# Expert weights split into three buffers, and another order of the head of a four-layer kernel

## What is computed

```python
x = x + ssm(layernorm(x))          # complex diagonal state space, 64 states, scan over 512 tokens, D skip, W_out, b_out
x = x + experts(layernorm(x))      # 8 experts, top 2 of a router
x = x + attention(layernorm(x))    # 16 heads of 64, bias by relative position, softmax
x = x + experts(layernorm(x))      # the same weights once more

def experts(x):                    # x: 2048 tokens x 128
    logits = x @ router_w.T
    vals, idx = top_k(logits, 2)
    g = sigmoid(vals); g = g / (g.sum(-1) + 1e-10)
    out = 0
    for e in range(8):
        ge = sum(where(idx == e, g, 0), -1)
        out += ge[:, None] * ((silu(x @ w_gate[e]) * (x @ w_up[e])) @ w_down[e])
    return out
```

## Time and profile before

| | us |
|---|---|
| median of 3 runs | 932.55 (930.68 to 934.95) |
| the profiled execution | 934.97 |
| its span in the profile | 933.2 |
| TensorE busy | 833.9 (89%) |
| VectorE, ScalarE, GpSimd busy | 645.2, 527.9, 432.1 |
| mean granted TensorE clock | 0.952 of 2.4 GHz |

### The profile page before, as it was taken

One profiled execution on the slowest core, in us unless ns is written; L12 is line 12 of the kernel. 1 busy time (PEld: TensorE's weight loads), 2 busy tenths in 40 slices (PEclk: granted clock), 3 DMA queues, 4 the chain that ended last, 5 costly groups with the idle time before them and its releaser, 6 DMA issues. The chain is left out here.

```text
span 933.2 us, 13407 instructions
## 1 busy us (share of the span) xinstructions
PE 833.9 (89%) x4320; PEld 559.7 (60%) x4320; DVE 645.2 (69%) x1600; ACT 527.9 (57%) x1161; POOL 432.1 (46%) x454
## 2 busy tenths in 40 slices
PE   2977878988789999999999999999999976899887
PEld 1566666866655556556565565565655565677665
DVE  7686666756778776767766768767688474775666
ACT  4445344544466766665666666666666543454443
POOL 2532568867324333332433424333335242697765
PEclk9878989989999999999999999999999997998999
DMA  6001263264000000000000000000000301622301
GB/s 203 3 1 25 62 120 88 60 195 189 0 1 1 1 1 1 1 1 1 1 2 1 1 1 1 1 2 1 23 13 1 70 1 42 120 83 57 85 1 45
DMA packets 51140, 35.14 MB, mean 38 GB/s; under 512 B 2640, under 2 KB 48592, under 8 KB 51072
## 3 DMA queue, kind: packets, MB, share of 16 engines
q1 hardware_dynamic: 51072, 34.30, 14.0%
HBM read 33.04 MB, written 1.25 MB: 37 GB/s over the span
## 5 line engine op out<-in xcount | busy, mean ns | idle before, releaser
L1200 POOL TENSOR_SCALAR prob<-prob,inv_total 128x512 f32<-128x512 f32 x256 | 175.0, 697 | 309.7 <-DVE inv_total L967 309.7
L720 POOL TENSOR_TENSOR hid_lo<-hid,hid_hi 128x512 fp32r<-128x512 f32 x128 | 190.6, 1504 | 153.7 <-ACT hid_hi L543 151.6
L1106 ACT ACTIVATE prob<-prob,peak 128x512 f32<-128x512 f32 x256 | 185.9, 726 | 46.4 <-DVE peak L978 46.4
L978 DVE CUSTOM_DVE_ANT_0 prob<-bank,bias_band 128x512 f32<-128x512 f32 x256 | 166.5, 688 | 28.8 <-PE bank L870 22.9
L597 DVE TENSOR_TENSOR hid<-silu,bank 128x512 f32<-128x512 f32 x128 | 87.3, 684 | 107.2 <-PE bank L245 89.3
L536 ACT ACTIVATE silu<-bank 128x512 f32<-128x512 f32 x128 | 76.4, 598 | 123.3 <-PE bank L245 123.3
L243 PE MATMUL bank<-xT_hi,w_hi 128*128 128x512 f32 x256 | 110.9, 433 | 36.4 <-POOL w_lo L710 29.8
L899 PE MATMUL bank<-probT,v 128*64 128x512 f32 x512 | 137.4, 617 | 0.0
L881 PE MATMUL bank<-ident,prob 128*128 128x128 f32 x1024 | 134.3, 274 | 3.0 <-ACT probT L1112 1.8
L881 PEld LDWEIGHTS bank<-ident,prob 128*128 128x128 f32 x1024 | 118.1, 141 | 21.6 <-issue 5.4
L624 DVE TENSOR_TENSOR hid<-hid,gate_all 128x512 f32<-128x512 f32 x118 | 120.5, 1023 | 8.5 <-DMA gate_all<-gates 0.7
(11 more groups left out here) (156 smaller groups left out, 1269.9 us busy)
## 6 DMA issues: line engine op xcount, KB each, us to landing
gate_all<-gates SPq DMA_DIRECT2D x59, 256.0 KB, 5.6
bias_band<-bias_rows SPq DMA_DIRECT2D x16, 448.0 KB, 8.8
w_raw<-in_w_gate SPq DMA_DIRECT2D x16, 128.0 KB, 2.3
w_raw<-in_w_up SPq DMA_DIRECT2D x16, 128.0 KB, 2.4
w_raw<-in_w_down SPq DMA_DIRECT2D x16, 128.0 KB, 2.5
x_res<-in_x SPq DMA_DIRECT2D x4, 256.0 KB, 5.2
out<-x_res SPq DMA_DIRECT2D x4, 256.0 KB, 2.3
wqT<-in_WqT SPq DMA_DIRECT2D x1, 512.0 KB, 6.1
```

The lines of the kernel that those rows point to most:

```text
L720: nc.gpsimd.tensor_tensor(m["hid_lo"][:, pos % 2, half, :], m["hid"][:, pos % deep, half, :], m["hid_hi"][:, pos % 2, half, :].bitcast(F32 ...
L978: nc.vector.tensor_tensor_reduce(out=prob[:, buf, h, :], in0=bank[2 * (n % 2) + h][:, :], in1=row_bias, scale=-1.0, scalar=NEG_START, op0= ...
L1106: nc.scalar.activation(prob[:, buf, h, :], prob[:, buf, h, :], ACT.Exp, bias=peak[:, buf, h:h + 1], scale=-1.0, accum_out=total[:, buf, h: ...
L1200: nc.gpsimd.tensor_scalar(prob[:, buf, h, :], prob[:, buf, h, :], inv[:, buf, h:h + 1], 1.0, ALU.mult, ALU.mult).then_inc(a_n, 1)
```

## The change

The weights get a third slot for `w_hi` and `w_lo` (`W_BUFS = 3`, expert e in slot e % 3; `w_raw` keeps two), each slot a tensor of its own at an address that is free at the time. `SPLIT_AT` gives the step at which the first of an expert's three pieces is split, the others follow in the next two. Steps are numbered 0 to 31 through a layer (`ORDER`), and `hid` is used four slots deep throughout. In the second expert layer chunk 3 comes later in the first eight steps. SyncE loads the gates of expert e + 2 behind the step that used their slot, and the next weights behind the third piece.

In the head the queues are reordered: loads of x first, the attention's weights in four loads with semaphores of their own, the first pair's layer norm ahead of the angles; PE turns wq first. The states make one product of both PSUM banks with cosine and sine together and one of the state with both; GpSimd's cosine product and bias go, the bias becomes a matmul of a row of ones (`ssm_skip`), in which the skip product also goes ahead of the states. The order on VectorE is states 0, 1, 2, residual 0, states 3, residual 1, layer norm of the first two chunks, residuals 2 and 3. The first eight expert steps and the routing are interleaved in another order, and in `leave` chunk 3's transpose, logits and gates come later.

The diff, cut to its core:

```diff
+        turn = slot(4, 2).rearrange("p (r s) -> p r s", r=2)
+        ut = slot(6, 2).rearrange("p (r s) -> p r s", r=2)
+        zt = slot(10, 4).rearrange("p (b r s) -> p b r s", b=2, r=2)
...
-                           w_raw=R(56), routing=R(62), gate_all=R(68)),
+                           w_hi=[R(44), R(47), R(84)], w_lo=[R(50), R(53), R(41)], w_raw=R(56), routing=R(62),
+                           gate_all=R(68)),
...
+        LAST_CHUNK_LATE = [(0, 0), (0, 1), (1, 0), (1, 1), (0, 2), (1, 2), (0, 3), (1, 3)]
+        ORDER = [[(2 * i + par_, c) for i, pair in enumerate([first, BY_EXPERT, BY_EXPERT, BY_CHUNK]) for par_, c in pair]
+                 for first in (BY_CHUNK, LAST_CHUNK_LATE)]
...
+        W_BUFS = 3
+        DEEP = 4
+        SPLIT_AT = [[None, None, 3, 6, 10, 14, 18, 22], [None, None, 3, 7, 10, 14, 18, 22]]
...
+        def splits(k, s):
+            return [(e, s - SPLIT_AT[k][e]) for e in range(2, E) if 0 <= s - SPLIT_AT[k][e] < 3]
-        FIRST_PIECES = {6: [(0, 1, 0)], 7: [(0, 1, 1)]}
-        MIDDLE_PIECES = {0: [(0, 0, 2)], 1: [(1, 0, 0)], 2: [(1, 0, 1)], 3: [(1, 0, 2)], 6: [(0, 1, 0)],
-                         7: [(0, 1, 1)]}
-        LAST_PIECES = {0: [(0, 0, 2), (1, 0, 0)], 1: [(1, 0, 1)], 2: [(1, 0, 2)]}
...
+            if e >= W_BUFS:
+                if piece < 2:
+                    act.wait_ge(q["u"], 2 * LAST[k][e - W_BUFS] + 2)
                 else:
+                    act.wait_ge(q["d"], LAST[k][e - W_BUFS] + 1)
...
         def experts_sync(sp, k):
+            for s in range(STEPS_K):
+                e, c = ORDER[k][s]
+                if e + 2 < E:
+                    sp.wait_ge(q["gm"], 2 * s + 2)
+                    load_gates(sp, k, e + 2, c)
+                for after in range(2, E - 2):
+                    if s == SPLIT_AT[k][after] + 2:
+                        load_weights(sp, k, after + 2)
...
+            def enter():
+                down(pe, 0, STEPS_K - 2)
                 ln_turn(pe, 2, 0, 4)
-                down_30()
...
             def leave():
                 part(2, 0)
                 pe.wait_ge(a_ea, SLOTS)
+                down(pe, 1, 0)
                 part(2, 1)
-                ln_turn(pe, 3, 3, JOB_BANK)
                 part(3, 0)
                 pe.wait_ge(a_eb, SLOTS)
+                down(pe, 1, 1)
                 part(3, 1)
+                ln_turn(pe, 3, 3, JOB_BANK)
+                part(4, 0)
+                pe.wait_ge(a_o, B * PAIRS)
+                down(pe, 1, 2)
+                part(4, 1)
                 route_logits(pe, 1, 3, JOB_BANK)
+                expert_step(pe, 1, 5)
+                expert_step(pe, 1, 6)
                 route_turn(pe, 1, 1)
                 route_spread(pe, 1, 3)
+                expert_step(pe, 1, 7)
...
+            def ssm_skip(b):
+                nc.tensor.matmul(bank[4 + b][:, :], ones[0:1, :], bo[0:1, :].unsqueeze(1).to_broadcast([1, QT, D]),
+                                 start=True, stop=False, skip_group_check=True)
+                for n in range(QT):
+                    nc.tensor.matmul(bank[4 + b][:, n * P:(n + 1) * P], xf[:, xtok], wd[:, :], start=False, stop=False,
...
+            for c in (2, 3):
+                pe.wait_ge(LN[0]["hi"], c - 1)
+                ln_turn(pe, 0, c, c + 2)
+            ssm_in(2)
+            ssm_skip(0)
+            ssm_out(0)
+            pe.wait_ge(LN[0]["hi"], 4)
+            ssm_in(3)
+            ssm_skip(1)
+            ssm_out(1)
...
+            step = lambda s: [gate_up(pe, 0, s, half) for half in range(2)]
             route_logits(pe, 0, 0, 4)
+            step(0)
             route_logits(pe, 0, 1, 5)
+            step(1)
+            step(2)
             ln_turn(pe, 1, 2, 6)
+            route_spread(pe, 0, 0)
+            route_spread(pe, 0, 1)
+            pe.wait_ge(m_x, 4)
+            route_turn(pe, 0, 0)
+            pe.wait_ge(MOE[0]["gt_c"], 1)
             ln_turn(pe, 1, 3, 7)
+            step(3)
...
-            def turn_back(b):
-                nc.gpsimd.tensor_tensor(zc[:, b % 2, :], z[:, b % 2, :], cosT, ALU.mult).then_inc(m_zc, 1)
...
+            layer_norm_0(0)
             dve.wait_ge(ld_times, 16)
...
+                nc.vector.tensor_tensor(ut, psum[:, 2 * (b % 2):2 * (b % 2) + 2, :], turn, ALU.mult).then_inc(m_z, 1)
+                nc.vector.tensor_tensor(ut[:, 0, :], ut[:, 0, :], ut[:, 1, :], ALU.add).then_inc(m_z, 1)
+                nc.vector.tensor_tensor(zt[:, b % 2], z[:, b % 2, :].unsqueeze(1).to_broadcast([P, 2, S]), turn,
+                                        ALU.mult).then_inc(m_zt, 1)
...
             states(0)
             states(1)
+            states(2)
             residual(0)
-            states(2)
+            states(3)
             residual(1)
-            states(3)
             dve.wait_ge(m_x, 2)
             ln_rows(dve, 1, 0, 2)
```

More of the change, by code:

```diff
@@ L561, in scalar_step @@
+        def scalar_step(act, k, s):
             silu_of(act, k, s, 0)
-            high_of(act, k, s - 1, (pos - 1) % 8, 1, deep_before if pos == 0 else deep)
+            high_of(act, k, s - 1, 1)
             silu_of(act, k, s, 1)
-            high_of(act, k, s, pos, 0, deep)
-            for par_, ahead, piece in pieces.get(pos, ()):
-                weight_high(act, k, i, par_, ahead, piece)
+            high_of(act, k, s, 0)
+            for e, piece in splits(k, s):
+                weight_high(act, k, e, piece)
@@ L632, in vector_step @@
+        def vector_step(dve, k, s):
             for half in range(MT):
-                product(dve, k, s, pos, half, deep, first and pos < deep)
-                gated(dve, k, i, order, pos, half, deep, first)
+                product(dve, k, s, half)
+                gated(dve, k, s, half)
         def add_sums(dve, k, c):
@@ L716, in low_of @@
             q, m = MOE[k], MEM[k]
             pool.wait_ge(q["hi"], 2 * s + half + 1)
-            if not first:
+            if s >= 2:
                 pool.wait_ge(q["d"], s - 1)
-            nc.gpsimd.tensor_tensor(m["hid_lo"][:, pos % 2, half, :], m["hid"][:, pos % deep, half, :],
-                                    m["hid_hi"][:, pos % 2, half, :].bitcast(F32), ALU.subtract).then_inc(q["hl"], 1)
-        def pool_step(pool, k, i, pos, pieces, deep=2, first=False):
-            s = 8 * i + pos
-            low_of(pool, k, s, pos, 0, deep, first and pos < 2)
-            for par_, ahead, piece in pieces.get(pos, ()):
-                weight_low(pool, k, 2 * (i + ahead) + par_, par_, piece)
-            low_of(pool, k, s, pos, 1, deep, first and pos < 2)
@@ L743, in build @@
+        def experts_pool(pool, k):
+            for s in range(STEPS_K):
+                low_of(pool, k, s, 0)
+                for e, piece in splits(k, s):
+                    weight_low(pool, k, e, piece)
+                low_of(pool, k, s, 1)
+        A_BANK = [6, 7, 6, 7]
         PV_BANK, JOB_BANK = 6, 7
@@ L1430, in _ @@
+            for piece in range(3):
+                weight_high(act, 0, 1, piece)
+            act.wait_ge(ld_wv, 16)
+            nc.scalar.copy(wvh[:, :], wv[:, :]).then_inc(s_ah, 1)
+            silu = lambda s: [silu_of(act, 0, s, half) for half in range(2)]
+            cast = lambda s: [high_of(act, 0, s, half) for half in range(2)]
             ln_apply(act, 1, 0, 0)
```

693 lines of the change are left out of this document (299 added, 394 removed).

## The result

The changed kernel takes 880.67 us (median; 873.09 to 881.91), the kernel before beside it 932.46: a ratio of 0.943 (95% interval 0.937 to 0.948). The forecast of 865 with 850 to 884 holds the time, but it is 15.7 us too low. Profile against profile, the spans went from 933.18 to 879.26 us, -53.9 where -68.3 had been summed.

A forecast was written before the change was run, and what follows sets the result against it. TensorE, busy 833.9 of 933.2 us, was taken as the bound, with idle and half-clock stretches to recover; -43.2 - 3.4 + 5.4 - 11.7 - 11 - 3 - 1.4 = -68.3 gave 864.3 against the median, say 865 us, range 850 to 884.

The forecast's parts named there:

- Edit 1: Expert layers: third weight buffer removes TensorE's waits for w_lo, -43.2 us in the steady stretches and -3.4 behind them.
- GpSimd behind it: Steady expert steps: GpSimd, 95% busy, could be late next; 0 taken, 10.4 us as the other end.
- Head: Before the first expert matmul: waits removed -10.7, cosine product +2.4, less stretching of VectorE -2.5; -11 us taken.
- Entry of the first layer: Start of the first expert layer: reordered steps and one long stop, -3 us, bounds +5 and -8.
- (d): Head's gain goes to TensorE's new order: residuals wait as before, plus the one long stop; 880 us, chance 0.10.
- Entry of the second layer: Start of the second expert layer: chunk 3 later cuts idle and low clock, -11.7 us, bounds -6 and -14.
- Gates on SyncE: Expert layers: first gate loads land late and queue, +5.4 us (4 beside 1.4).
- Into the attention: Before the attention: the last but one down product goes first, into TensorE's 3.32 us idle for x_norm; -1.4 us.
- (b): Expert layers: the clock does not come back, only the idle 29.8 of 43.2 is gained; 882 us, chance 0.08.
- (e): Expert steps: slower than before because the two-slot hid ring binds; above 937 us, chance 0.01.
- (a): Steady expert steps: GpSimd takes the place of the wait for weights; 875 us, chance 0.12.
- (c): Both expert layers: the gate loads' burst binds steps 8 to 10, 8 and 4 us more; 877 us, chance 0.12.

The follow-up runs named there:

- edit 6: Last but one down product put ahead of the third layer's first transpose, part of the changed kernel; undone alone there: 876.96 us, ratio 0.940.
- the doubled low parts: Changed kernel with GpSimd making each low part of the weights from expert 2 on twice: 893.15 us, ratio 0.960.
- the second entry: Changed kernel with VectorE making the last chunk's gate weights and picks ahead of step 5 in the second expert layer: 877.92 us, ratio 0.942.
- three orders: First-entry reorderings of silu and products, gate weights and picks, and gates' copy, on the changed kernel; together with all other reorderings: 862.45 us, ratio 0.925.
- the first two: Changed kernel, first entry: silu and products of step 4 earlier, 876.24 us; then also gate weights and picks ahead of gated products, 875.45 us.

## Why the prediction was right in sign and range, and 15.7 us low

The time lies in the range, but the inner band of the forecast, 856 to 874, was missed by 6.7 us. The large term was right in its mechanism; the misses are in the small ones.

- **Edit 1 (43.2 + 3.4).** Right: 41.6 + 3.8 by the stretches; with two slots the same four stretches are 45.9 us longer, the whole run 41.6. The step that paid was to price the stretch by windows and not by its idle alone: 16.8 of these us were matmuls at the lower level (13.4 + 3.4 had been worked out). The Trainium skill, "TensorE: Matmul & The Clock Gate", part 1, puts the ramp penalty at under 1% of a typical kernel span, in a passage on the slow matmuls at a kernel's start; the prediction set it against ramps behind waits. Here it is no bound for those: the 16.8 us are 1.8% of the span of 933.18 from this one cause.
- **GpSimd behind it (0 taken, 10.4 as the end).** Right, with 1.2 us in 33.5 to spare: the two stretches took 75.96 and 75.39 us where 18 undisturbed steps are 74.9, so at most 1.6 us in place of the 10.4.
- **Head (-11, measured -7.4).** The failed step is the contention term, by which "VectorE's stretched ones (up to 2.28 for eight elements) mostly go": -2.5. They grew: 7.7 us beside GpSimd's qk_lo, w_lo and wv_lo against some 5.6 before, so the term was +2.1 instead of -2.5. The text named those three pieces and still took a gain. The states' products with both inputs in SBUF were moved forward to where these subtractions run, and the run with GpSimd later shows 7.2 us of delay on VectorE's chain, and 2.2 to 5.0 on TensorE's (its start of step 0 at 52.05 against 54.29 to 57.05). The removed waits (10.7) were right: no residual waited.
- **Entry of the first layer (-3, and +2 for gates; measured +0.8).** The failed step is the list of what stands ahead of step 4 on ScalarE: a cast that waits for a gate load, an exponential and two table loads of 1.28 us, which the sum priced at nothing. The single long stop behind step 2 (rival (d), second half) was 2.33 us at x_norm, as expected; the 4.47 us at 89.63 was not foreseen.
- **Entry of the second layer (-11.7, and +3.4 for gates; measured -8.5, and -10.0 in a second execution).** Right in sum. In its parts not quite: the gates' wait was 3.12 us where 1.4 had been worked out; three of the weights' small instructions took 1.26, 0.66 and 0.94 us beside GpSimd instead of some 0.17, which is 2.3 us. The loads cost TensorE nothing there.
- **Gates on SyncE (+5.4).** VectorE waited 5.9 us for loads, 3 times, with 1.71 in the second layer where 4 had been taken. In the first layer 3.34 of them fed the stop at 89.63. The term is inside the two entries.
- **Into the attention (-1.4, measured +1.6).** Wrong in sign. The sum counted the wait that the down product fills and not the one that it leaves: it had stood in the wait behind the transpose. Undone, the stretch is 1.5 to 2.6 us shorter. Of the +1.6 some 1.1 is this execution's longer low stretch: six of the nine profiles with edit 6 are 0.5 to 0.6 above the kernel before.
- **Attention and end (0, measured +3.7 and +1.4).** Not effects of the change. At the end the mean clock was 0.78, against 0.97 before; the same kernel's last execution took 15.6 us there with no slow matmul, as long as before, and its variants took 15.6 to 17.2 with the same code.
- **Rivals.** (b) is out by the two-slot run, (e) and (f) by the traces; (a) and (c) are the next bounds, shown by the doubled low parts and the second entry. The misses that count, in the head, at the first entry and on the way into the attention, had no rival of their own; (d) expected the head to lose 7 us to residuals that wait for TensorE, and none waited.

## What to carry to other kernels

Before work is moved into a gap, ask which gap it leaves: a filled wait moves, and the matmuls behind the emptied one may run at half clock. When a list of one engine is reordered, list what of the neighbour that shares its access to SBUF runs at the same time, and keep GpSimd's uncritical work out of VectorE's critical stretch. When an edit removes a wait and the time stays, follow the stop through the other engines' queues before it is called useless: here three orders, with the head's, gave 4.7 to 6 us, and the first two 1 at most.

## What the runs showed of the hardware

**VectorE and GpSimd take turns.** A VectorE product with both inputs in SBUF that starts while a GpSimd subtraction runs isn't slowed by a share; it ends only after that is over. GpSimd's ends at 20.68 + 2.36 = 23.04, VectorE's 0.69 us product at 23.59; the next pair at 29.46 and 30.00; wv_lo at 44.33 and the 1.22 us product at 45.42. GpSimd pays too: three w_lo took 4.45 us there and 2.10 alone. It holds through the whole trace of the changed kernel: 64 of the products with the gate (L616) start inside a GpSimd subtraction, and all 64 end 0.55 to 0.63 us after its end, while the 96 products with an input in PSUM (L596) that start inside one take 0.67 to 0.69 us. Even instructions of eight elements go from 0.17 to 0.66 to 1.26 us: the cast that starts at 753.91 ends at 755.17, the subtraction beside it (753.33 + 1.82) at 755.15. The Trainium skill, "Trainium Architecture — The Big Picture", section "What this means for kernel authors", calls this pair's port an exclusive lock and no split of bandwidth; the ends above agree with it. I had read the averages (0.99 instead of 0.69) as a mild tax, which they are only when many short instructions are averaged.

**An idle of 1.7 to 2.0 us may or may not cost the clock.** The same code with the same idles took 480.7 to 485.9 us in the attention, by the number of its low stretches. So 2 to 5 us between two executions of this kernel are no evidence for an edit, and two stretches should be compared by their granted clock before their length.
